# Matmul operands 32 bytes off, or on, a multiple of 64 in SBUF: three weight tensors and one activation tensor moved in a gated attention block

## What is computed

```python
x = x + tanh(g_xattn[0]) * attn(layernorm(x), ctx, ctx)
x = x + tanh(g_ffn[0]) * (einsum('bsi,oi->bso', layernorm(x), weight * scale_weight[:, None]) + bias)

def attn(q, k, v):                        # H = 16 heads of HD = 32
    Q = (q @ Wq.T + bq).reshape(bs, sl, H, HD)        # K and V likewise, from ctx
    score = einsum('bshd,bsgd->bshg', Q, K)           # heads against heads, within one token
    attn = einsum('bshg,bsgd->bshd', softmax(score), V).reshape(bs, sl, 512)
    return attn @ Wo.T + bo
```

## The kernel before

| layer | stationary, bytes past a multiple of 64 | moving, likewise | form |
|---|---|---|---|
| K, Q | weights, 0 | ctx, x1, 32 | 128x256 |
| V, O | ctx, x1, 32 | wv, wo, 0 | 128x512 |
| F | x2, 32 | wf, 0 | 128x512 (last tile 128x256) |
| transposes | `ident` 0 and `x_norm` or `v_or_norm` 32 | | 128x128 |
| `keep_clock`, 12 matmuls at the start | `ident`, 0 | `ident`, 0 | 128x128 |

## Time and profile before

### The profile page before, as it was taken

One profiled execution on the slowest core, in us unless ns is written; L12 is line 12 of the kernel. 1 busy time (PEld: TensorE's weight loads), 2 busy tenths in 40 slices (PEclk: granted clock), 3 DMA queues, 4 the chain that ended last, 5 costly groups with the idle time before them and its releaser, 6 DMA issues.

```text
span 297.7 us, 8697 instructions
## 1 busy us (share of the span) xinstructions
PE 275.5 (93%) x3556; PEld 241.6 (81%) x3556; DVE 191.7 (64%) x329; ACT 143.8 (48%) x273; POOL 88.9 (30%) x81
## 2 busy tenths in 40 slices
PE   7899896688959999999999999999999999789896
PEld 7789885676937899888988899889988899578675
DVE  2785376287784687439754787459664772398974
ACT  4655628841593033672378034833287135834500
POOL 4203004006193024323180326231271136004531
PEclk9999999599997999999999999999999999999999
DMA  7997595994843652739565853757473623862102
GB/s 202 357 363 213 197 187 188 240 240 90 294 127 92 124 211 104 182 81 205 208 165 117 168 184 141 163 142 176 153 200 82 146 102 118 195 103 92 46 25 108
DMA packets 65113, 48.60 MB, mean 163 GB/s; under 512 B 36288, under 2 KB 54464, under 8 KB 65088
## 3 DMA queue, kind: packets, MB, share of 16 engines
q1 hardware_dynamic: 65088, 48.25, 58.6%
HBM read 31.46 MB, written 16.78 MB: 162 GB/s over the span
## 4 chain that ended last, share of the span: by engine, by line
PE 66%; DVE 9%; DMA 9%; SPq 6%; issue 5%; POOL 2%; ACT 1%; DVEq 0%; POOLq 0%
PE acc L449 54%; PE turn_ps L483 4%; PE score_ps L567 3%; DMA q_scratch<-q_t 3%; DMA late<-wv_t 3%; DMA x_res<-x 3%; PE score_ps L449 2%; PE attn_ps L589 2%; DVE v_or_norm L866 1%; SPq L340 1%; DVE stats L844 1%; DMA q_pad<-q_scratch 1%; POOL x_res L1131 1%; DVE wf_parts L830 1%; DVE late L966 1%
## 5 line engine op out<-in xcount | busy, mean ns | idle before, releaser
L449 PE MATMUL acc<-ctx_parts,wk_parts 128*128 128x256 f32 x384 | 48.7, 286 | 0.4 <-ACT wk_parts L662 0.4
L449 PEld LDWEIGHTS acc<-ctx_parts,wk_parts 128*128 128x128 f32 x384 | 47.5, 193 | 1.7 <-issue 0.5
L737 ACT ACTIVATE late<-attn_ps 32x256 f32<-32x256 f32 x120 | 45.1, 376 | 6.7 <-PE attn_ps L589 3.9
L449 PE MATMUL acc<-wv_parts,ctx_parts 128*128 128x512 f32 x192 | 46.9, 399 | 1.1 <-ACT wv_parts L662 1.1
L449 PE MATMUL acc<-xa_parts,wq_parts 128*128 128x256 f32 x384 | 46.4, 280 | 1.4 <-DVE late L980 1.4
L449 PEld LDWEIGHTS acc<-xa_parts,wq_parts 128*128 128x128 f32 x384 | 45.5, 188 | 2.0 <-issue 1.8
L1120 POOL TENSOR_TENSOR rstd<-var_eps,minus_half 128x1 f32<-128x1 f32 (+1 forms) x24 | 16.2, 673 | 101.7 <-DVE var_eps L855 101.7
L449 PEld LDWEIGHTS acc<-wv_parts,ctx_parts 128*128 128x128 f32 x192 | 35.4, 188 | 9.2 <-issue 1.3
L449 PE MATMUL acc<-wo_parts,xa_parts 128*128 128x512 f32 x168 | 40.9, 399 | 1.0 <-ACT xa_parts L662 1.0
L449 PEld LDWEIGHTS acc<-wo_parts,xa_parts 128*128 128x128 f32 x168 | 31.1, 188 | 9.1 <-ACT xa_parts L662 1.5
L449 PE MATMUL acc<-wf_parts,x_parts 128*128 128x512 f32 (+1 forms) x132 | 32.0, 400 | 4.1 <-DVE v_or_norm L897 4.1
(11 more groups left out here) (81 smaller groups left out, 369.4 us busy)
## 6 DMA issues: line engine op xcount, KB each, us to landing
ctx_raw<-ctx_t SPq DMA_DIRECT2D x8, 512.0 KB, 4.3
x_norm<-x SPq DMA_DIRECT2D x8, 512.0 KB, 5.6
k_scratch<-k_t SPq DMA_DIRECT2D x8, 512.0 KB, 2.8
k_rows<-k_scratch SPq DMA_DIRECT2D x32, 128.0 KB, 3.4
v_scratch<-v_or_norm SPq DMA_DIRECT2D x32, 128.0 KB, 2.2
q_scratch<-q_t SPq DMA_DIRECT2D x8, 512.0 KB, 3.8
q_pad<-q_scratch SPq DMA_DIRECT2D x32, 128.0 KB, 3.3
v_keys<-v_scratch SPq DMA_DIRECT2D x16, 256.0 KB, 5.4
```

The costliest lines, as they stand in the source:

```text
L449: last = pe.matmul(dst, left(a, k), right(b, k), start=(n == 0), stop=(n == len(terms) - 1))
L737: nc.scalar.activation(attn_rows(t, q), attn_block(t, q), ACT.Identity).then_inc(a_out, 1)
```

## The change

No instruction is added, taken away or moved on any engine, and no wait changes. Three tiles of 32 bytes that nobody reads are put between others, and the five weight tiles are asked for in another order:

```diff
-        weights = {n: sb(f"{n}_parts", [P, 2, KC, D], F32R) for n in ("wv", "wq", "wk", "wo", "wf")}
+        shift = 32 // 4
+        weights = {n: sb(f"{n}_parts", [P, 2, KC, D], F32R) for n in ("wq", "wk")}
+        sb("shift_moving", [P, shift])
+        weights |= {n: sb(f"{n}_parts", [P, 2, KC, D], F32R) for n in ("wv", "wo", "wf")}
+        sb("shift_back", [P, shift])
         ident = sb("ident", [P, P])
...
         xa_parts = sb("xa_parts", [P, 2, KC, TOK], F32R)
+        sb("shift_x2", [P, shift])
         x2_parts = sb("x2_parts", [P, 2, KC, TOK], F32R)
         q_t, k_t = sb("q_t", [P, GROUPS, KC, GT]), sb("k_t", [P, GROUPS, KC, GT])
```

## The result

The changed kernel takes 301.82 us (median of 22 runs) against 300.97 for the kernel before (22 runs on the same chips): a ratio of 1.0048, with a 95% interval of 1.0027 to 1.0069. So it is half a per cent slower, by more than the measurement is uncertain, and the forecast of no change was wrong. That the forecast of 301.5 lies so near 301.8 is in part luck: it was set on the median of three runs, 301.58, and 22 runs of the same kernel give 300.97. The sign could be told, and the reason is not one that the prediction considered.

A forecast was written before the change was run, and what follows sets the result against it. The prediction took TensorE to bound the middle, with DMAs among the waits at both ends. Every term was 0, leaving the profiled execution at 299.4 us; with the median 2.16 above it, it said 301.5 us, range 297.5 to 303.2.

The forecast's parts named there:

- forecast of no change: Whole kernel: the placement does nothing, time within about 0.3% of before; chance 0.50.
- What bounds the kernel: Middle steps of 33 us: TensorE busy for all 33.00, so each nanosecond per matmul is a nanosecond of the kernel.
- the count of the tail: End of the chain: 24 matmuls of O and some 52 of F, within 264 of V and O and 172 of F.
- the same (64 bytes further on): K and Q's placement, taken as unmoved modulo 64; the sum has no term for them.
- K's and Q's 117: Sign in the profile after: K's and Q's pitch in a middle step stays 117 ns.
- For each moving column both pay exactly the same: Big matmuls before: K and F, with opposite placements modulo 64, both pay 0.456 ns for each moving column.
- V and O as a like pair: V and O, both operands 32 off a multiple of 64 after the change: pitch change taken as 0.
- F: F, operands' placement exchanged: 0 to 3.2 ns gain per 512-column matmul, 0 to 0.55 us in all; taken as 0.
- The first: Rival on V, O and F: moving operand's placement sets the 22 ns; 292 at the far end; chances 0.13 large, 0.12 small.
- The collision rival: V and O: stationary and moving operand, now placed alike, collide; 0.6 to 1.2 us slower, 302.7; chance 0.17.
- The DMA rival: q_scratch and q_pad DMAs on the chain: aligned tiles land earlier, 0.9 to 3.3 us gain, 300.2; chance 0.08.
- estimate of 13%: DMAs on the chain, from the skill page: 13% of q_pad's time and 4% of q_scratch's, some 0.8 us gain.

The follow-up runs named there:

- `plus64`: The kernel before with one tile of 64 bytes added behind the weights, nothing changed modulo 64; 304.47 us, ratio 1.0124.
- `weights_follow`: Every tile modulo 256 as in the changed kernel, but wk and wq 64 bytes further on; 299.30 us, ratio 0.9953 to the kernel before.
- `order_only`: The kernel before with only the weight tiles reordered to wq, wk, wv, wo, wf, no tile of 32 bytes; 300.49 us, ratio 1.000.

## Why the prediction was wrong, point by point

**What bounds the kernel.** Right: a middle step is TensorE alone, and a pitch passes through. Five stretches of +0.31 us are on the chain as they stand. In the count of the tail a slip was made that changes nothing: "some 52" of F takes the two x12 of the last tile as whole, and with halves counted as halves there are 40, so F has 160 and the three layers 424.

**K and Q.** This is the step that failed. The prediction's table of placements, and with it the sum, took a start modulo 64 for all that a placement is, so K and Q had no term: "the same (64 bytes further on)". They had the only one. 3.2 ns on the 480 of their matmuls in the five x120 is 1.5 us, 0.5%, as measured (0.48%); another 96 on the chain lie before 40 us, where their 0.3 us are made up for. "K's and Q's 117" was one of the signs that the prediction named for itself, and it is the one that failed: they have 120. `plus64` shows that those 64 bytes alone bring the 120 ns and `weights_follow` that undoing the distance by the other operand undoes it.

**"For each moving column both pay exactly the same."** The reading of before was right, 0.456 ns in K, Q and F. The inference, that placement therefore has no part in it, was not: two different distances, 32 at 256 columns and 224 at 512, happen to give the same rate. Two equal numbers at two settings were taken for independence of the setting.

**V and O as a like pair.** The term of 0 was right: 233.3 before and after. But the reason was wrong. The pair (32, 32) of the change has distance 192, and a like pair at distance 0 gains 4 to 7 ns (226.6 to 229.4).

**F.** 0 to 3.2 ns of gain were allowed; it lost 0.9 (234.2), some 0.15 us.

**The rivals.** The first, that a part of the 22 ns above half the slow pitch can be had by placement, has a true core: 4 to 7 of them are won at distance 0 (there are 20, for the starts at the half clock are 426 or 427 ns apart and not 423), but not by the moving operand's own place, and not in this change. The collision rival named the right two parties, the stationary and the moving operand, but looked at their places modulo 64 and so put it on the wrong layers. The DMA rival was right for one transfer of three: v_keys lands 1.0 us sooner (5.4 to 4.4), but the prediction did not have it on the chain, and the two that it had there are as short without the alignment. Of the rule in the Trainium skill's DMA: Bandwidth & Descriptors, How a descriptor splits into AXI transactions, the trace agrees in direction for v_keys, whose pieces of 128 bytes started 160 past a multiple of 256, so that every second one lay across it; for q_pad's pieces of 1,024 bytes, of which the prediction made its estimate of 13%, no run here shows it.

What stays open: why the distance counts at all (no run shows where the two operands get in each other's way), why one placement has two or three pitches and which of them a layer falls into, whether the tiles behind x2 are worth any time, and why the clock fell more often in some kernels' executions than in others'.

## What to carry to other kernels

When a tile is added, enlarged or moved, compare the starts of both operands of the hot matmuls, as a distance modulo 256, before and after; a padding tile that leaves everything "aligned as it was" modulo 64 can cost half a per cent and more. Read a pitch from the starts of two layers, for each layer apart, since a busy share of 93% says nothing about it. And where two settings give the same number, that is no proof that the setting does not count.

## What the runs showed of the hardware that was not expected

At the full granted clock (2.4 GHz) the pitch of a float32r matmul with another weight load under it depends on the distance of its two operands in SBUF: 113.3 to 120.1 ns for 128x256 and 226.6 to 234.3 for 128x512; at 1.2 GHz it is 213 or 214 and 426 or 427 in all the placements tried.

What the distance of K and Q alone is worth in time can be read from two kernels. `weights_follow` and the changed kernel differ in the place of wk and wq (and in the order of the weight tiles, which `order_only` shows to be worth nothing). At a mean clock of 0.981 to 0.983 their medians are 299.30 us (11 runs) and 301.39 (12), 0.7%, taken on different chips; by their ratios, 0.9953 and 1.0048, it would be 0.9%, but those carry the clock with them. The changed kernel's own loss is not a matter of the clock: at that clock the kernel before has medians of 299.69 to 300.24 us in the experiments above, so 0.4 to 0.6% less. But a ratio of half a per cent is near what another mix of clocks makes, and the two have to be read side by side.
